# Attention loop: the middle query tiles taken in pairs, with PSUM bank pairs rotating between logits and transposes

## The chip, the core and the metric

One Trainium2 chip, one NeuronCore of it. The engines named here are TensorE (PE in the rows, its weight loads PEld), VectorE (DVE), ScalarE (ACT), GpSimd (POOL) and SyncE (SP, which issues DMAs). The metric is the device time of one execution in microseconds (us), as the median of several runs.

## What is computed

A transformer block: attention with a residual, then a mixture of experts with a residual. Only the attention is touched:

```python
x = x + _layernorm(_L0_attn_ref(_layernorm(x, axis=-1), L0_attn_w_qkv, L0_attn_w_proj, L0_attn_b_proj), axis=-1)
x = x + _layernorm(_L0_ffn_ref(_layernorm(x, axis=-1), ...), axis=-1)
# attention, x is (8, 1024, 256)
qkv = jnp.einsum('bse,he->bsh', x, w_qkv)
q, k, v = jnp.split(qkv, 3, axis=-1)
scores = jnp.einsum('bqh,bkh->bqk', q, k) * scale
probs = jax.nn.softmax(scores, axis=-1)
out = jnp.einsum('bqk,bkh->bqh', probs, v)
out = jnp.swapaxes(out, 1, 2).reshape(Bn, Sn, H)
out = jnp.einsum('bsh,eh->bse', out, w_proj) + b_proj
```

## The kernel before

The program first runs eight attention rounds, one for each batch entry of 1024 tokens (`r` = 0 to 7; rounds 3 to 6 are a hardware loop over one body, the others are written out), and then the mixture of experts. The rounds take the span from about 18 to 564 us. All order is written by hand: each engine runs its own `body(R)` in program order and the engines meet at counting semaphores (`wait(engine, semaphore, value)`).

A round begins on TensorE with 24 matmuls for `tT` (the queries times the folded weights), from round 1 on 48 matmuls of the last round's output projection, and 48 matmuls for V. Then come the eight query tiles of 128 rows. For one query tile `i` the work is a chain over three engines. All products are made of three matmuls (`mm3`: high times high, high times low, low times high), so each result in PSUM is split by ScalarE (high part) and VectorE (low part).

- **logits(i)**: 12 matmuls of 128x512 on TensorE (L60 to L62) into a pair of PSUM banks. Called S below.
- **largest(i)**: VectorE, negated row maximum of the 1024 logits (L710).
- **exp(i)**: ScalarE, exponent with row sum (L555, and a short row that reads the accumulator), into `Pr`.
- **turn(i)**: 8 transposes of 128x128 on TensorE (L442) into a pair of banks. Called P below.
- **hi(i), lo(i)**: ScalarE copies the high part in two halves (L548), VectorE makes the low part in two halves (L723).
- **value product(i)**: 8 matmuls of 128x512 (L453, needs hi(i)) and 8 of 128x256 (L458, needs lo(i)), into `psO` or `psL`. Called H and L below.
- **o_sum(i)** on VectorE (L705), **o_hi(i)** on ScalarE (L543), **o_lo(i)** on VectorE (L716): the output tile, in this order, each waiting for the one before.

Before, logits used `psS` (bank pairs 1 and 0 in turn) and the transposes always used `psPT` (bank pair 2). The steps run one tile at a time, so TensorE's row of work in a round is S0 S1 P0 S2 P1 H0L0 S3 P2 H1L1 S4 P3 H2L2 S5 P4 H3L3 S6 P5 H4L4 S7 P6 H5L5 P7 H6L6 H7L7.

Between the steps each engine does side work of the round:

- ScalarE, rounds 2 to 7: `join` (L487) in steps 2 and 3. Rounds 1 to 7: `norm_y` (L471) in steps 3 and 4.
- VectorE: `ln_y` (statistics of the projected output, rounds 1 to 7) in steps 0 to 2, `gate_scores` (rounds 2 to 7) in step 1, `ln_next` (statistics of the next batch entry, rounds 0 to 6) in steps 2 and 3, `ln_x1` (statistics of x after the attention, rounds 1 to 7) in steps 5 and 6.
- GpSimd: in this order, a chain of small operations after `ln_y` (which lets `norm_y` start), one after `ln_next` (L765 to L775), and then `add_x` (L747), two additions of 1024 columns, of which the first waits for the first `norm_y` and the second for the second. `ln_x1` part 0 waits for the first addition (semaphore `s_x1`), part 1 for the second.
- Round 0 has none of `ln_y`, `norm_y`, `join`, `gate_scores`, `ln_x1`, but splits three shared weights (`shared_hi` on ScalarE, L219, then `shared_lo` on VectorE, L224, which waits for it) in steps 1, 2 and 6, and centres one in step 5.

Of the kernel before, what the change touches and what calls it, by code (L numbers as in the profile page):

```python
# [227 lines left out]
def attention(nc, io, c):  # L228
    with ExitStack() as ctx:
# [75 lines left out]
        def logit_bank(i):  # L305
            return 2 - 2 * (i % 2)
# [60 lines left out]
        def _(pe):  # L367
# [13 lines left out]
            def body(R):  # L381
# [42 lines left out]
                for step in range(NT + 2):  # L424
                    i0, i1, i2 = step, step - 1, step - 2
                    if i0 < NT:
                        b = logit_bank(i0)
                        if i0 < 2:
                            wait(pe, s_vl, 4 * r + 2 * i0 + 2)
                        else:  # L430
                            wait(pe, s_exp, 8 * r + i0 - 1)
                        for n in range(2):
                            for kk in range(KD):
                                w = [tT[z][:, kk, i0 * P:(i0 + 1) * P] for z in (0, 1)]
                                x = [xnT[z][:, kk, n * 512:(n + 1) * 512] for z in (0, 1)]
                                i = mm3(pe, psS[:, b + n, :], w[0], w[1], x[0], x[1], kk == 0, kk == KD - 1)
                        i.then_inc(s_s, 1)
                    def turn_p():
                        wait(pe, s_exp, 8 * r + i1 + 1)
                        wait(pe, s_ptl, 2 * (8 * r + i1))  # L440
                        for t in range(NT):
                            i = pe.transpose(psPT[:, t * P:(t + 1) * P], Pr[:, i1 % 2, t * P:(t + 1) * P], c.ident[:, :])  # L442
                            if t % 4 == 3:
                                i.then_inc(s_t, 1)

                    def output(ts):
                        if ts[0] == 0:
                            wait(pe, s_pth, 2 * (8 * r + i2 + 1))
                            wait(pe, s_os, 8 * r + i2 - 1)
                            if i2 == 0:  # L450
                                wait(pe, s_vl, 4 * (r + 1))
                        for t in ts:
                            pe.matmul(output_bank(i2)[:, :], PT[0][:, i2 % 2, t, :], V_both[:, t, :, :].rearrange("p z d -> p (z d)"),  # L453
                                      start=(t == 0), stop=False)
                        for t in ts:
                            if t == 0:
                                wait(pe, s_ptl, 2 * (8 * r + i2 + 1))
                            i = pe.matmul(output_bank(i2)[:, 0:D], PT[1][:, i2 % 2, t, :], V[0][:, t, :], start=False, stop=(t == NT - 1))  # L458
                        i.then_inc(s_pv, 1)

                    if 0 <= i1 < NT:
                        turn_p()
                    if i2 >= 0:
                        output(range(NT))
# [3 lines left out]
        def _(a):  # L468
# [45 lines left out]
            def body(R):  # L514
# [21 lines left out]
                for step in range(NT + 3):  # L536
                    i0, i1, i3 = step, step - 1, step - 3
                    if i3 >= 0:
                        if i3 == 0:
                            wait(a, s_y, 4 * r)  # L540
                        wait(a, s_ri, 8 * r + i3 + 1)
                        wait(a, s_os, 8 * r + i3 + 1)
                        a.activation(O[0][:, i3, :], Osum[:, i3 % 2, :], ACT.Copy, scale=rinv[:, i3:i3 + 1]).then_inc(s_oh, 1)  # L543
                    if 0 <= i1 < NT:
                        wait(a, s_pv, 8 * r + i1 - 1)
                        for h in range(2):
                            wait(a, s_t, 2 * (8 * r + i1) + h + 1)
                            a.activation(PT[0][:, i1 % 2, 4 * h:4 * h + 4, :],  # L548
                                         psPT[:, h * 512:(h + 1) * 512].rearrange("p (t c) -> p t c", t=4),
                                         ACT.Copy).then_inc(s_pth, 1)  # L550
                    if i0 < NT:
                        wait(a, s_max, 8 * r + i0 + 1)
                        wait(a, s_t, 2 * (8 * r + i0 - 1))
                        b = logit_bank(i0)
                        a.activation(Pr[:, i0 % 2, :], psS[:, b:b + 2, :].rearrange("p a c -> p (a c)"), ACT.Exp,  # L555
                                     bias=negmax[:, i0:i0 + 1], accum_out=rowsum[:, i0:i0 + 1]).then_inc(s_exp, 1)
# [8 lines left out]
                    if R.post and step in (3, 4):  # L565
                        norm_y(r, step - 3)
                    if isinstance(r, int) and r == 0 and step in (1, 2, 6):
                        setup.shared_hi(a, (1, 2, 6).index(step))
            rounds(a, body)

        def aggregate(v, n):
            v.drain()
# [16 lines left out]
        def _(v):  # L589
# [30 lines left out]
            def body(R):  # L620
# [75 lines left out]
                def task(step, side):  # L696
                    if (step, side) in tasks:
                        f, part = tasks[step, side]
                        f(part)
# [1742 lines left out]
```

## Time and profile before

| | us |
|---|---|
| median of 3 runs (1948.04 to 1949.56) | 1948.2 |
| the profiled execution | 1948.25 |
| its span, first to last instruction | 1946.2 |
| PE busy in the span | 1919.5 |
| DVE busy | 1368.9 |
| ACT busy | 1036.9 |
| POOL busy | 521.9 |

Busy times are sums over the whole span. Matmuls overlap in the rows, because the time of one runs from its start to its modelled end, so what tells how fast TensorE goes is the distance from start to start. A round's times are given on the clock of this profile. Round 5, used as the example, has its first logits at 374.84 us and hands over to round 6 at 426.41 us.

### The profile page before, as it was taken

Reading aid. Unit: us, or ns where it says so; the run is one execution under the profiler, and the core shown is the slowest. Engines: PE = TensorE matmul, PEld = TensorE weight load, DVE = VectorE, ACT = ScalarE, POOL = GpSimd, SP = SyncE. Lnnn points to the kernel's source line nnn. Section 1 sums busy time; section 2 is a strip of 40 time slices with the busy share of each in tenths; the row PEclk is TensorE's granted clock in tenths of the full one; section 3 lists DMA queues with packets and bytes.
Section 4 is the critical chain, followed back from the end, with each engine's and each line's share of the span. In section 5 each row is a group of like instructions: output and inputs, shape, how many; then the busy total and the mean of one; then the engine's idle time right before and its main releaser. Section 6 shows DMA issues by size and latency. Waiting matters only on the chain.

```text
span 1946.2 us, 29069 instructions
## 1 busy us (share of the span) xinstructions
PE 1919.5 (99%) x10608; PEld 1647.2 (85%) x10608; DVE 1368.9 (70%) x2619; ACT 1036.9 (53%) x1929; POOL 521.9 (27%) x611
## 2 busy tenths in 40 slices
PE   8999999999999999999999999999999999999996
PEld 6888888888888888888888888888888888888886
DVE  6777787777776888767677777656565756565647
ACT  5457576675655445445454544545454545455455
POOL 0031132033030000322432333243234323432146
PEclk9999999999999999999999999999999999999998
DMA  3113323324244111444434443444434443434566
GB/s 131 55 33 101 86 100 109 97 78 139 52 157 155 66 61 43 136 82 104 92 89 106 94 99 81 107 87 110 87 97 99 91 105 92 105 85 107 152 216 173
DMA packets 153338, 197.37 MB, mean 101 GB/s; under 512 B 104449, under 2 KB 121089, under 8 KB 145153
## 3 DMA queue, kind: packets, MB, share of 16 engines
q1 hardware_dynamic: 127824, 158.00, 26.1%
q0 software_dynamic: 25392, 37.77, 12.2%
q8 instruction: 74, 1.21, 0.2%
q14 instruction: 48, 0.39, 0.1%
HBM read 114.38 MB, written 59.34 MB: 89 GB/s over the span
## 4 chain that ended last, share of the span: by engine, by line
PE 66%; POOL 2%; DVE 1%; DMA 1%; issue 0%; ACT 0%; DVEq 0%; POOLq 0%
PE mo_psD L1637 12%; PE mo_psG L60 7%; PE mo_psU L60 7%; PE mo_psG L61 7%; PE mo_psG L62 7%; PE mo_psU L62 7%; PE mo_psU L61 7%; PE mo_psD L1642 6%; PE mo_psD L60 1%; PE mo_psD L61 1%; PE mo_psD L62 1%; DMA out_dram<-mo_F 1%; POOL mo_H_lo L2296 1%; PE mo_psX L1359 1%; POOL mo_rs L2306 0%
## 5 line engine op out<-in xcount | busy, mean ns | idle before, releaser
L1774 ACT ACTIVATE mo_HF<-mo_psG 128x512 f32<-128x512 f32 x320 | 191.8, 599 | 375.9 <-PE mo_psU L62 344.2
L2278 POOL DMA_INDIRECT ACC<-OUT,IDX x128 | 201.7, 1576 | 623.8 <-DVE OUT L2069 612.3
L1986 DVE TENSOR_TENSOR mo_HF<-mo_psU,mo_HF 128x512 f32<-128x512 f32 x320 | 220.4, 689 | 187.1 <-ACT mo_HF L1774 180.4
L1637 PE MATMUL mo_psD<-wd,mo_H_hi 128*128 128x512 f32 x1024 | 256.3, 392 | 0.3 <-DVE OUT L2069 0.3
L60 PE MATMUL mo_psG<-mo_XT_hi,wg_hi 128*128 128x512 f32 x640 | 253.7, 396 | 0.6 <-DVE mo_HF L1986 0.5
L60 PE MATMUL mo_psU<-mo_XT_hi,wu_hi 128*128 128x512 f32 x640 | 249.9, 390 | 0.0
L61 PE MATMUL mo_psG<-mo_XT_lo,wg_hi 128*128 128x512 f32 x640 | 249.8, 390 | 0.0
L62 PE MATMUL mo_psG<-mo_XT_hi,wg_lo 128*128 128x512 f32 x640 | 249.3, 390 | 0.0
L62 PE MATMUL mo_psU<-mo_XT_hi,wu_lo 128*128 128x512 f32 x640 | 249.0, 389 | 0.0
L61 PE MATMUL mo_psU<-mo_XT_lo,wu_hi 128*128 128x512 f32 x640 | 249.0, 389 | 0.0
L1637 PEld LDWEIGHTS mo_psD<-wd,mo_H_hi 128*128 128x128 f32 x1024 | 185.7, 188 | 35.2 <-DVE OUT L2069 0.5
L1896 DVE TENSOR_TENSOR mo_H_lo<-mo_HF,mo_H_hi 128x512 fp32r<-128x512 f32 x304 | 207.8, 683 | 0.0
L1733 ACT ACTIVATE mo_H_hi<-mo_HF 128x512 fp32r<-128x512 f32 x318 | 198.0, 623 | 8.5 <-DVE mo_HF L1986 8.5
L2069 DVE SCALAR_TENSOR_TENSOR OUT<-mo_psD,mo_TW,OUT 128x256 f32<-128x256 f32 x128 | 61.9, 484 | 185.9 <-ACT OUT L1832 185.9
L1832 ACT ACTIVATE OUT<-mo_psD,mo_TW 128x256 f32<-128x256 f32 x128 | 60.8, 475 | 239.7 <-PE mo_psD L1642 239.7
L1642 PEld LDWEIGHTS mo_psD<-wd,mo_H_lo 128*128 128x128 f32 x1024 | 141.1, 189 | 10.6
L1642 PE MATMUL mo_psD<-wd,mo_H_lo 128*128 128x256 f32 x1024 | 144.1, 284 | 0.0
L60 PEld LDWEIGHTS mo_psG<-mo_XT_hi,wg_hi 128*128 128x128 f32 x640 | 120.2, 188 | 27.8 <-DVE mo_HF L1986 4.3
L62 PEld LDWEIGHTS mo_psG<-mo_XT_hi,wg_lo 128*128 128x128 f32 x640 | 120.1, 188 | 25.7
L60 PEld LDWEIGHTS mo_psU<-mo_XT_hi,wu_hi 128*128 128x128 f32 x640 | 120.1, 188 | 25.3
L62 PEld LDWEIGHTS mo_psU<-mo_XT_hi,wu_lo 128*128 128x128 f32 x640 | 120.1, 188 | 25.1
L61 PEld LDWEIGHTS mo_psU<-mo_XT_lo,wu_hi 128*128 128x128 f32 x640 | 120.2, 188 | 24.8
(356 smaller groups left out, 3981.6 us busy)
## 6 DMA issues: line engine op xcount, KB each, us to landing
X1a<-wg_in SPq DMA_DIRECT2D x16, 1024.0 KB, 4.8
X1a<-wu_in SPq DMA_DIRECT2D x16, 1024.0 KB, 4.9
X1a<-wd_in SPq DMA_DIRECT2D x16, 1024.0 KB, 4.8
XN<-XG SPq DMA_DIRECT2D x8, 1088.0 KB, 4.1
X<-x_in SPq DMA_DIRECT2D x8, 1024.0 KB, 5.4
out_dram<-X SPq DMA_DIRECT2D x8, 1024.0 KB, 6.3
XN2T<-xn2T SPq DMA_DIRECT2D x8, 1024.0 KB, 5.1
X1a<-xt_in SPq DMA_DIRECT2D x7, 1024.0 KB
```

The lines of the kernel that those rows point to most:

```text
L60: pe.matmul(out, w_hi, x_hi, start=first, stop=False)
L61: pe.matmul(out, w_hi, x_lo, start=False, stop=False)
L62: return pe.matmul(out, w_lo, x_hi, start=False, stop=last)
L1637: pe.matmul(psD[:, t % 2, :], hidden(b, it)[0][:, t * P:(t + 1) * P], wd_both[:, it, :, :].rearrange("p z d -> p (z d)"), start=(it == 0), ...
L1642: i = pe.matmul(psD[:, t % 2, 0:D], hidden(b, it)[1][:, t * P:(t + 1) * P], wd[0][:, it, :], start=False, stop=(it == n - 1))
L1733: a.activation(hidden(b, it)[0], HF[:, it % 2, :], ACT.Copy).then_inc(s_hhi, 1)
L1774: a.activation(HF[:, it % 2, :], psG[:, it % 2, :], ACT.Gelu).then_inc(s_gelu, 1)
L1832: i = a.activation(OUT[:, t, :], psD[:, t % 2, 0:D], ACT.Copy, scale=scale)
L1896: v.tensor_tensor(lo, HF[:, it % 2, :], hi.bitcast(F32), ALU.subtract).then_inc(s_hlo, 1)
L1986: v.tensor_tensor(HF[:, it % 2, :], psU[:, it % 2, :], HF[:, it % 2, :], ALU.mult).then_inc(s_mul, 1)
L2069: v.scalar_tensor_tensor(OUT[:, t, :], psD[:, t % 2, D:2 * D], TW[n % 2][:, 4 * tb + t:4 * tb + t + 1], OUT[:, t, :], ALU.mult, ALU.add).t ...
L2278: g.indirect_dma_start(out=io["ACC"], out_offset=bass.IndirectOffsetOnAxis(ap=c.IDX[:, n, 4 * tb + t:4 * tb + t + 1], axis=0), in_=OUT[:, ...
```

## The change

The order inside a round is written out anew on TensorE, ScalarE and VectorE; the bank pair of each logits and each transpose comes from a table. Nothing is computed differently and no operation is added or removed. The middle query tiles go in pairs. TensorE's row of work is now S0 S1 P0 S2 H0L0 P1 P2, then S3 S4 H1L1 H2L2 P3 P4, then S5 S6 H3L3 H4L4 P5 P6, then S7 H5L5 P7 H6L6 H7L7. Logits use bank pairs 1 0 1 1 2 2 0 0, transposes 2 2 0 0 1 1 2 2. With it the waits change: S4 and S6 now wait for lo(1) and lo(3) (`s_ptl`), because they write the banks that these read; of the transposes only the odd ones wait for the lo of the tile before.

The side work keeps its step numbers as arguments of `tasks` (ScalarE) and `task` (VectorE), with one change of place: `ln_x1` part 0 stands alone in step 5, parts 1 and 2 in step 6.

```diff
-        def logit_bank(i):
-            return 2 - 2 * (i % 2)
+        LOGIT_BANKS = [bank_pairs[i] for i in (1, 0, 1, 1, 2, 2, 0, 0)]
+        TURN_BANKS = [bank_pairs[i] for i in (2, 2, 0, 0, 1, 1, 2, 2)]
...
+                def logits(i):
+                    if i < 2:
+                        wait(pe, s_vl, 4 * r + 2 * i + 2)
+                    elif i in (4, 6):
+                        wait(pe, s_ptl, 2 * (8 * r + i - 2))
+                    else:
+                        wait(pe, s_exp, 8 * r + (1 if i == 2 else i))
...
+                def turn_p(i):
+                    wait(pe, s_exp, 8 * r + i + 1)
+                    if i in (1, 3, 5, 7):
+                        wait(pe, s_ptl, 2 * (8 * r + i))
...
+                logits(0)
+                logits(1)
+                turn_p(0)
+                logits(2)
+                output(0)
+                turn_p(1)
+                turn_p(2)
+                for i in (3, 5):
+                    logits(i)
+                    logits(i + 1)
+                    output(i - 2)
+                    output(i - 1)
+                    turn_p(i)
+                    turn_p(i + 1)
+                logits(7)
+                output(5)
+                turn_p(7)
+                output(6)
+                output(7)
             rounds(pe, body)
...
+                exp(0)
+                turned_p(0)
+                exp(1)
+                tasks(1)
+                exp(2)
+                tasks(2)
+                o_hi(0)
+                turned_p(1)
+                turned_p(2)
+                tasks(3)
+                for i in (3, 5):
+                    exp(i)
+                    tasks(4 if i == 3 else 6)
+                    exp(i + 1)
+                    o_hi(i - 2)
+                    o_hi(i - 1)
+                    turned_p(i)
+                    turned_p(i + 1)
+                exp(7)
+                tasks(7)
+                o_hi(5)
+                turned_p(7)
+                tasks(8)
...
             rounds(a, body)
...
-                              (5, 0): (ln_x1, 0), (5, 1): (ln_x1, 1), (6, 0): (ln_x1, 2)}
+                              (5, 0): (ln_x1, 0), (6, 0): (ln_x1, 1), (6, 1): (ln_x1, 2)}
...
+                largest(0)
+                task(0)
+                largest(1)
+                turned_p(0)
+                task(1)
+                if R.gate:
+                    gate_scores()
+                largest(2)
+                task(2)
+                o_sum(0)
+                o_lo(0)
+                turned_p(1)
+                turned_p(2)
+                task(3)
+                for i in (3, 5):
+                    largest(i)
+                    if i == 5:
+                        task(6)
+                    largest(i + 1)
+                    if i == 3:
+                        task(5)
+                    o_sum(i - 2)
+                    o_lo(i - 2)
+                    o_sum(i - 1)
+                    o_lo(i - 1)
+                    turned_p(i)
+                    turned_p(i + 1)
+                largest(7)
+                task(7)
+                o_sum(5)
+                o_lo(5)
+                turned_p(7)
...
             rounds(v, body)
```

The first place is TensorE in round 2, after the transposes of tile 0 and the logits of tile 2. Before:

```order
L442 MATMUL psPT<-ident,Pr 128x128 [waits s_ptl,s_exp]
L442 MATMUL psPT<-ident,Pr 128x128 x7
L453 MATMUL psO<-V,PT_hi 128x512 [waits s_vl,s_os,s_pth]
L453 MATMUL psO<-V,PT_hi 128x512 x7
L458 MATMUL psO<-V,PT_lo 128x256 [waits s_ptl]
L458 MATMUL psO<-V,PT_lo 128x256 x7
```

After, on the same engine at the same place:

```order
L453 MATMUL psO<-V,PT_hi 128x512 [waits s_vl,s_os,s_pth]
L453 MATMUL psO<-V,PT_hi 128x512 x7
L457 MATMUL psO<-V,PT_lo 128x256 [waits s_ptl]
L457 MATMUL psO<-V,PT_lo 128x256 x7
L443 MATMUL psPT<-ident,Pr 128x128 [waits s_ptl,s_exp]
L443 MATMUL psPT<-ident,Pr 128x128 x7
L443 MATMUL psS<-ident,Pr 128x128 [waits s_exp]
L443 MATMUL psS<-ident,Pr 128x128 x7
```

The value product of tile 0 moved ahead of the transposes of tile 1, and the transposes of tile 2 follow at once, ahead of the logits of tile 3.

The second place is VectorE in round 2, from largest(2) (the first row) to the low part of tile 2 (the last row). Before:

```order
L710 TENSOR_REDUCE negmax<-psS 128x1 [waits s_s]
L720 RECIPROCAL rinv<-rowsum 128x1 [waits s_exp]
L723 TENSOR_TENSOR PT_lo<-psPT,PT_hi 128x512 [waits s_pth] x2
L574 BN_AGGR mv<-st 128x2 x8
L581 BN_STATS st<-X 128x6 [waits s_x]
L581 BN_STATS st<-X 128x6 x3
L705 TENSOR_REDUCE Osum<-psO 128x256 [waits s_pv]
L710 TENSOR_REDUCE negmax<-psS 128x1 [waits s_s]
L716 SCALAR_TENSOR_TENSOR O_lo<-Osum,rinv,O_hi 128x256 [waits s_oh]
L720 RECIPROCAL rinv<-rowsum 128x1 [waits s_exp]
L723 TENSOR_TENSOR PT_lo<-psPT,PT_hi 128x512 [waits s_pth] x2
```

After:

```order
L759 TENSOR_REDUCE negmax<-psS 128x1 [waits s_s]
L615 BN_AGGR mv<-st 128x2 x8
L622 BN_STATS st<-X 128x6 [waits s_x]
L622 BN_STATS st<-X 128x6 x3
L749 TENSOR_REDUCE Osum<-psO 128x256 [waits s_pv]
L754 SCALAR_TENSOR_TENSOR O_lo<-Osum,rinv,O_hi 128x256 [waits s_oh]
L764 RECIPROCAL rinv<-rowsum 128x1 [waits s_exp]
L767 TENSOR_TENSOR PT_lo<-psPT,PT_hi 128x512 [waits s_pth] x2
L764 RECIPROCAL rinv<-rowsum 128x1 [waits s_exp]
L767 TENSOR_TENSOR PT_lo<-psS,PT_hi 128x512 [waits s_pth] x2
```

The low part of tile 1 moved behind o_sum(0) and o_lo(0), and stands together with that of tile 2.

The third place is VectorE later in round 2, around the wait for GpSimd's addition (`s_x1`). Before, the rows end with the second part of `ln_x1`:

```order
L705 TENSOR_REDUCE Osum<-psO 128x256 [waits s_pv]
L710 TENSOR_REDUCE negmax<-psS 128x1 [waits s_s]
L716 SCALAR_TENSOR_TENSOR O_lo<-Osum,rinv,O_hi 128x256 [waits s_oh]
L720 RECIPROCAL rinv<-rowsum 128x1 [waits s_exp]
L723 TENSOR_TENSOR PT_lo<-psPT,PT_hi 128x512 [waits s_pth] x2
L581 BN_STATS st<-X 128x6 [waits s_x1]
L581 BN_STATS st<-X 128x6 x3
L581 BN_STATS st<-X 128x6 [waits s_x1]
L581 BN_STATS st<-X 128x6 x3
```

After, from largest(3) on:

```order
L759 TENSOR_REDUCE negmax<-psS 128x1 [waits s_s]
L759 TENSOR_REDUCE negmax<-psPT 128x1 [waits s_s]
L622 BN_STATS st<-X 128x6 [waits s_x1]
L622 BN_STATS st<-X 128x6 x3
L749 TENSOR_REDUCE Osum<-psL 128x256 [waits s_pv]
L754 SCALAR_TENSOR_TENSOR O_lo<-Osum,rinv,O_hi 128x256 [waits s_oh]
L749 TENSOR_REDUCE Osum<-psO 128x256 [waits s_pv]
L754 SCALAR_TENSOR_TENSOR O_lo<-Osum,rinv,O_hi 128x256 [waits s_oh]
L764 RECIPROCAL rinv<-rowsum 128x1 [waits s_exp]
L767 TENSOR_TENSOR PT_lo<-psS,PT_hi 128x512 [waits s_pth] x2
```

The wait for `s_x1` stood behind the low part of tile 4 and now stands behind largest(4), ahead of o_sum(1) and of everything for tiles 1 to 4 that follows on VectorE.

## Rows read from the trace of the kernel before

**Rows 1.** The page: busy time of the engines, and the chain that ended last.

```profile
PE 1919.5 (99%) x10608; PEld 1647.2 (85%) x10608; DVE 1368.9 (70%) x2619; ACT 1036.9 (53%) x1929; POOL 521.9 (27%) x611
...
PE 66%; POOL 2%; DVE 1%; DMA 1%; issue 0%; ACT 0%; DVEq 0%; POOLq 0%
```

**Rows 2.** Timeline, TensorE, round 5: start us, us, then the operation.

```profile
380.46 1.09 PE L442 MATMUL psPT<-ident,Pr 128*128 128x128 f32 x8
381.31 0.48 PE L60 MATMUL psS<-xnT_hi,tT_hi 128*128 128x512 f32 x1
...
384.14 1.03 PE L442 MATMUL psPT<-ident,Pr 128*128 128x128 f32 x8
384.93 2.08 PE L453 MATMUL psO<-V,PT_hi 128*128 128x512 f32 x8
386.85 1.13 PE L458 MATMUL psO<-V,PT_lo 128*128 128x256 f32 x8
387.81 0.39 PE L60 MATMUL psS<-xnT_hi,tT_hi 128*128 128x512 f32 x1
...
390.56 1.03 PE L442 MATMUL psPT<-ident,Pr 128*128 128x128 f32 x8
391.35 2.08 PE L453 MATMUL psL<-V,PT_hi 128*128 128x512 f32 x8
...
423.60 2.01 PE L453 MATMUL psL<-V,PT_hi 128*128 128x512 f32 x8
425.44 1.13 PE L458 MATMUL psL<-V,PT_lo 128*128 128x256 f32 x8
```

**Rows 3.** Timeline, ScalarE, round 5: exp(0), exp(2), first `join`, o_hi(0).

```profile
379.12 1.12 ACT L555 ACTIVATE Pr<-psS,negmax 128x1024 f32<-128x1024 f32 x1 [3.20 <-DVE negmax L710]
...
386.82 1.12 ACT L555 ACTIVATE Pr<-psS,negmax 128x1024 f32<-128x1024 f32 x1 [0.95 <-DVE negmax L710]
...
387.92 2.58 ACT L487 ACTIVATE xn2T<-xn_turned 128x1024 uint16<-128x1024 uint16 x2
390.77 0.51 ACT L543 ACTIVATE O_hi<-Osum,rinv 128x256 fp32r<-128x256 f32 x1 [0.27 <-DVE Osum L705]
```

**Rows 4.** Timeline, VectorE, round 5: lo(1), `ln_next`, largest(4), `ln_x1`, o_sum(5), o_lo(5).

```profile
386.77 1.27 DVE L723 TENSOR_TENSOR PT_lo<-psPT,PT_hi 128x512 fp32r<-128x512 f32 x2
...
395.03 0.64 DVE L574 BATCH_NORM_AGGREGATE mv<-st 128x2 f32<-128x6 f32 x8
...
397.18 1.23 DVE L710 TENSOR_REDUCE negmax<-psS 128x1 f32<-128x1024 f32 x1 [0.94 <-PE psS L62]
...
406.58 2.70 DVE L581 BATCH_NORM_STATS2 st<-X 128x6 f32 x8
...
420.46 0.68 DVE L705 TENSOR_REDUCE Osum<-psL 128x256 f32<-128x512 f32 x1
421.78 0.49 DVE L716 SCALAR_TENSOR_TENSOR O_lo<-Osum,rinv,O_hi 128x256 fp32r<-128x256 f32 x1 [0.64 <-ACT O_hi L543]
```

**Rows 5.** Timeline, GpSimd, round 5: first row of the `ln_next` chain, both additions.

```profile
395.76 0.20 POOL L765 TENSOR_TENSOR ve<-mv,eps 128x8 f32<-128x8 f32 x1 [2.58 <-DVE mv L574]
...
399.60 2.41 POOL L747 TENSOR_TENSOR X<-X,X1a 128x1024 f32 x1 [0.39 <-issue]
402.38 2.38 POOL L747 TENSOR_TENSOR X<-X,X1a 128x1024 f32 x1 [0.37 <-ACT X1a L471]
```

**Rows 6.** Timeline, ScalarE and VectorE, round 0: the second shared weight's split.

```profile
43.07 1.05 ACT L219 ACTIVATE wu_hi<-XG 128x1024 fp32r<-128x1024 f32 x1
...
44.15 1.23 DVE L224 TENSOR_TENSOR wu_lo<-XG,wu_hi 128x1024 fp32r<-128x1024 f32 x1 [0.97 <-ACT wu_hi L219]
```

**Rows 7.** Stretches: length, busy us of PE, PEld, DVE, ACT, POOL, then PEclk, DMA, GB/s.

```profile
564.28:566.63 2.35, 0.17 (x2) 0.03 (x1) 1.19 (x3) 0.51 (x1) 0.04 (x1) 1.00 0.00 0
567.50:571.00 3.50, 3.50 (x19) 3.50 (x18) 0.46 (x1) 3.25 (x7) 0.09 (x2) 0.52 0.92 286
615.50:619.00 3.50, 3.50 (x19) 3.50 (x19) 0.38 (x2) 1.76 (x3) 0.00 (x0) 0.53 0.02 5
```

More of the change, by code:

```diff
@@ L423, in body @@
                     i.then_inc(s_v, 1)
[L424 to L464, printed above, removed]
@@ L535, in body @@
                     a.activation(SM[:, :, :], SM[:, :, :], ACT.Exp).then_inc(s_sme, 1)
[L536 to L556, printed above, removed]
@@ L557, in body, with o_hi, tasks @@
+                def o_hi(i):
+                    if i == 0:
+                        wait(a, s_y, 4 * r)
+                    wait(a, s_ri, 8 * r + i + 1)
+                    wait(a, s_os, 8 * r + i + 1)
+                    a.activation(O[0][:, i, :], Osum[:, i % 2, :], ACT.Copy, scale=rinv[:, i:i + 1]).then_inc(s_oh, 1)
+                def tasks(step):
                     if R.gate and step in (2, 3):
@@ L729, in body, with task @@
+                def task(step):
                     if isinstance(r, int) and r == 0 and step in (1, 2, 6):
@@ L732, in body, with o_sum @@
                         setup.center(v)
-                    task(step, 0)
-                    task(step, 1)
-                    if step == 1 and R.gate:
-                        gate_scores()
+                    for side in range(2):
+                        if (step, side) in tasks:
+                            f, part = tasks[step, side]
+                            f(part)
+                def o_sum(i):
+                    wait(v, s_pv, 8 * r + i + 1)
+                    v.tensor_reduce(Osum[:, i % 2, :], output_bank(i)[:, :].rearrange("p (z d) -> p d z", z=2), AX.X,
+                                    ALU.add).then_inc(s_os, 1)
@@ new lines, in turned_p @@
+                def turned_p(i):
+                    wait(v, s_exp, 8 * r + i + 1)
+                    v.reciprocal(rinv[:, i:i + 1], rowsum[:, i:i + 1]).then_inc(s_ri, 1)
+                    for h in range(2):
+                        wait(v, s_pth, 2 * (8 * r + i) + h + 1)
+                        v.tensor_tensor(PT[1][:, i % 2, 4 * h:4 * h + 4, :], TURN_BANKS[i][:, h, :].rearrange("p (t c) -> p t c", t=4),
+                                        PT[0][:, i % 2, 4 * h:4 * h + 4, :].bitcast(F32), ALU.subtract).then_inc(s_ptl, 1)
@@ L737, in _ @@
+                largest(7)
[3 more added lines that the diff above has]
+                turned_p(7)
+                if R.ln_next:
+                    scale_next(1)
+                    scaled_lo(r + 1, (0, 1))
+                o_sum(6)
+                if R.ln_next:
+                    scaled_lo(r + 1, (2, 3))
+                o_lo(6)
+                o_sum(7)
+                o_lo(7)
             rounds(v, body)
```

76 lines of the change are left out of this document (44 added, 32 removed).

## The prediction

> **What bounds the kernel now.** I read the page first. TensorE is busy for 1919.5 of 1946.2 us, and the chain that ended last is TensorE's for 66%, with no other engine above 2% [rows 1]. That share alone doesn't say that TensorE never waits, because matmuls overlap in the rows. So I read next the timeline of TensorE in round 5, for the distance from start to start. One step there is 12 logit matmuls in 2.75 us (387.81 to 390.56), 8 transposes in 0.79 (to 391.35), and a value product of about 1.92 and 0.96 us [rows 2], 6.42 us in all, and the steps from tile 3 to tile 7 repeat with it. Logits that follow logits take 2.73. So TensorE runs back to back, and only the first transposes of a round wait: S0 starts at 374.84 and two logits take 5.46, to 380.30, while P0 starts at 380.46 [rows 2]. The other engines have room: ScalarE waited 0.95 us before exp(2) and VectorE 0.94 us before largest(4) [rows 3, 4]. Anything that makes TensorE wait is therefore paid in full, and anything that lets the others run faster gives nothing.
>
> **What the pairs can give.** The matmuls are the same. Only the changes from one kind to another differ. A first half of a value product behind transposes takes 1.92 (384.93 to 386.85), behind a value product 1.84 (423.60 to 425.44) [rows 2]: 0.08 each, seven times a round before and once now, 0.45 saved. Logits behind a value product cost 0.02 more than 2.73, five times before and never now, 0.10 saved. Logits behind transposes cost 0.10 more (381.31 to 384.14 is 2.83) [rows 2], taken as 0.11 with the other rounds, once before and four times now, 0.33 lost. Net 0.22 us a round, 1.8 us in eight. Two new neighbours are not in the trace. A value product behind logits lies between 1.84 and 1.92; I take 1.84, since both are the same kind of matmul. Transposes behind transposes I take at the 0.79 of transposes behind logits. With the other ends, the gain is gone and 0.6 us is lost.
>
> **What the new order delays.** VectorE, ScalarE and GpSimd work strictly in their written order, so I laid the new order out by hand from the distances in the rows, for a middle round on the clock of round 5. First the distances: exp is ready for TensorE 1.34 us after its start (379.12 to 380.46) and lets ScalarE go on after 1.10 (386.82 to 387.92) [rows 2, 3]. largest takes 1.23, and the next VectorE row can start 1.14 after it; a pair of low parts takes 1.2; o_lo starts 1.32 after o_sum (420.46 to 421.78), because o_hi on ScalarE lies between them, and lets go after 0.4 [rows 4]. The same distances applied to the old order give a round without any wait but the one before P0, as the trace has it.
>
> *P2 waits for exp(2): 0.44 us.* Up to exp(2) nothing changes, as the work ahead of largest(2) on VectorE is the same. exp(2) starts at 386.8 and is ready at 388.1. Before, TensorE had P1, a value product and S3 ahead of P2, and was there at 390.56. Now it has one value product and P1: S2 ends at 384.1, H0L0 2.80, P1 0.79, so it arrives at 387.7.
>
> *S4 waits for lo(1): 0.96 us.* Lo(1) stood at 386.77, directly behind largest(2) [rows 4]. Now o_sum(0) and o_lo(0) come first, and o_lo(0) needs o_hi(0), which stands behind `join` on ScalarE: 387.92 and two of about 1.2 us, so o_hi(0) starts at 390.3, o_lo(0) at 390.85, lo(1) at 391.35 and its second half is ready at 392.7. S3 starts at 388.9 and ends at 391.7.
>
> *S6 waits for lo(3): 3.12 us.* This is the large one. On GpSimd, the chain after `ln_next` begins when VectorE's aggregate is done (395.03, 0.64 long, then 395.76) and leads to the first addition at 399.60, 3.84 us later, which lasts 2.41 [rows 4, 5]. In the new order the aggregate starts 0.3 us later, so the first addition runs from 399.9 to 402.3. Before, VectorE asked for it at 406.58 [rows 4], 4.6 us after it was there (399.60 + 2.41). Now it asks right behind largest(4): largest(3) at 395.9, largest(4) at 397.0, done with at 398.1. VectorE stands for 4.2 us, and queued behind the wait are o_sum(1), o_lo(1), o_sum(2), o_lo(2), lo(3) and lo(4). From 402.3: `ln_x1` part 0 is half of 2.70 (1.33), to 403.7; o_sum(1), o_lo(1), 1.72, to 405.4; o_sum(2), o_lo(2), to 407.1; the small reciprocal; lo(3) halves at 407.2 and 407.8, ready at 408.57. TensorE is done with H1L1 H2L2 P3 P4 S5 at 405.45 and waits for the bank pair that lo(3) reads. Behind S6 the round has slack again. P7 comes only 2.8 us after S7, and largest(7) and exp(7) take 0.2, 1.25 and 1.34, which is the same 2.8: no stall, but nothing to spare.
>
> **The sum.** Rounds 2 to 6 have all three: 4.52 each, less 0.22, is 4.30, or 21.5 for five. Round 1 has no `join` and no `gate_scores`, so all comes earlier by more than the first two waits and only S6's is left, 2.47: net 2.2. Round 7 has no `ln_next`, so GpSimd goes straight to the addition, which then waits for the first `norm_y` (behind both `join`s): P2 0.44, S4 0.96, S6 0.44: net 1.6. Round 0 has the shared weights instead. A split of 1024 columns takes ScalarE 1.05 us and VectorE 1.23, and VectorE's waits for ScalarE's [rows 6]. In task(2) it now stands between largest(2) and o_sum(0), so VectorE waits 2.3 us there for exp(2) and the ScalarE copy behind it: P2 0.33, S4 2.88, P7 0.34: net 3.4. Together 21.5 + 2.2 + 1.6 + 3.4 = 28.7 us. The mixture of experts starts behind the last round's value product as before, so nothing absorbs this.
>
> *The clock.* From 564.28 to 566.63 TensorE stood nearly idle, 2.35 us, with transposes behind, and in the stretch 567.5 to 571 the granted clock is 0.52, which is the lower level of 1.2 GHz for almost all of 3.5 us [rows 7]. That costs up to 3.5 times 0.48, 1.7 us. Seven of the new stalls are at least as long (S4 of round 0, S6 of rounds 1 to 6). The bounds are 0 and 7 x 1.7 = 11.9 us. That one stall had transposes behind it, and mine have logits at once, so not each will be followed by a drop; I take two or three, 4.2 us.
>
> Forecast: 28.7 + 4.2 = 32.9 on 1948.25 of the profiled execution, which is the median of 1948.2 within 0.05: **1981 us**.
>
> **Rivals.**
> *The rotation works as drawn.* If S4 and S6 find their banks free and P2 its exponents, only the 1.8 us of neighbours are left: 1946.4, no measurable change. For it speaks that TensorE had no wait before and the others had room; against it, the 4.6 us by which VectorE's request for the addition was late before, and is early now. The Trainium skill (Perfetto Trace Analysis, section Optimizing Tensor Performance, Matmuls) says that independent groups of matmuls should rotate through different PSUM banks, so that emptying one overlaps the next group. By that rule this rival would hold. The trace of before does not contradict it, but it shows that the emptying engine has other waits in its queue, of which the rule says nothing.
> *The stalls, and no drop of the clock:* 1977. *The stalls, and a drop at each of the seven:* 1989. In the second a slow S6 also makes largest(6) late by a few tenths.
> *The other side.* The trace has a second stretch at the lower clock soon after the first, 615.5 to 619, about as long [rows 7]. If the new timing moves both starts so that neither drops, 2 x 1.7 and the 1.8 make 5.2 us: 1943. This needs the waits to be absent as well; the point from which it decides is that P2, S4 and S6 wait for less than 3.4 us in all eight rounds together.
>
> **How the numbers follow.** Forecast with two to four drops (1979 to 1985) 0.5; none or one 0.22; five or more 0.14; rotation as drawn 0.06; smaller stalls than worked out, for 1952 to 1972, 0.05; the other side 0.03. About 0.2%, or 4 us, is what a measurement of this kernel can tell from no change. So faster 0.03, same 0.06, slower 0.91. The range goes from 1972, five below the case without drops for errors in the distances, to 1991, two above the case with all.
>
> **What would show it.** In the new trace TensorE's starts in rounds 2 to 6 should show P2 late by 0.4 us, S4 by 1.0 and S6 by 3.1; VectorE should be idle some 4.2 us before `ln_x1` part 0, released by GpSimd's addition (L821); each round should last about 4.3 us longer than 69.0 (374.84 to 443.83, from first logits to first logits), round 1 2.2, round 0 3.4. Right behind S6 the granted clock tells about the drops. I am wrong if VectorE doesn't wait for the addition, or if S6 starts right behind S5.

## The result

| | before | changed |
|---|---|---|
| median | 1948.21 us (1948.04 to 1949.56) | 1986.96 us (1984.21 to 1988.04) |
| the profiled execution, its span | 1948.25, 1946.2 | 1987.87, 1985.8 |
| PE busy in the span | 1919.5 | 1934.0 |
| mean granted clock of TensorE | 0.996 | 0.991 |

The ratio is 1.0196, 95% interval 1.0184 to 1.0208. The changed kernel is 38.75 us slower, the forecast was 32.9 (1981, range 1972 to 1991). The traces used below are each of one execution, which need not be the one with the median time.

### The profile after

The page, parts 1 and 4, as in [rows 1]: TensorE's work is the same in count, and the chain that ended last is still TensorE's for 66%.

```profile
PE 1934.0 (97%) x10608; PEld 1655.1 (83%) x10608; DVE 1371.7 (69%) x2619; ACT 1035.1 (52%) x1929; POOL 522.4 (26%) x611
...
PE 66%; DVE 2%; ACT 0%; DVEq 0%; issue 0%; POOL 0%; ACTq 0%; POOLq 0%
```

That part looks almost as before and says nothing of the cause. The list of waits does. TensorE's in the attention (18 to 606 us; engine, line waited for: us in total, times, longest):

```profile
PE psS L60 <- DVE PT_lo L767: 16.7, 7, 3.1
```

A second row of the same kind, for logits into `psPT`, has 7.3 us, seven times, 2.7 at most. TensorE's timeline of round 5 shows where these lie, and is read by starts against [rows 2]. P1 and P2, S3, S4, H1, P3 and P4, S5, S6, H3:

```profile
411.66 1.03 PE L443 MATMUL psPT<-ident,Pr 128*128 128x128 f32 x8
412.89 1.09 PE L443 MATMUL psS<-ident,Pr 128*128 128x128 f32 x8 [0.19 <-ACT Pr L553]
413.74 0.48 PE L60 MATMUL psS<-xnT_hi,tT_hi 128*128 128x512 f32 x1
...
417.50 0.50 PE L60 MATMUL psPT<-xnT_hi,tT_hi 128*128 128x512 f32 x1 [0.78 <-DVE PT_lo L767]
...
420.36 1.98 PE L453 MATMUL psL<-V,PT_hi 128*128 128x512 f32 x8
...
425.95 1.91 PE L443 MATMUL psS<-ident,Pr 128*128 128x128 f32 x16
427.62 0.48 PE L60 MATMUL psPT<-xnT_hi,tT_hi 128*128 128x512 f32 x1
...
433.66 0.53 PE L60 MATMUL psS<-xnT_hi,tT_hi 128*128 128x512 f32 x1 [3.05 <-DVE PT_lo L767]
434.00 0.61 PE L61 MATMUL psS<-xnT_lo,tT_hi 128*128 128x512 f32 x1
434.41 0.63 PE L62 MATMUL psS<-xnT_hi,tT_lo 128*128 128x512 f32 x1
...
438.12 1.98 PE L453 MATMUL psL<-V,PT_hi 128*128 128x512 f32 x8
```

- P1 and P2 take 2.08 us from start to start (411.66 to 413.74). A pair that waits for nothing takes 1.67 (P3 and P4, 425.95 to 427.62). So P2 is 0.41 late.
- S3 to S4 is 3.76 where 12 logit matmuls behind transposes take 2.83 (381.31 to 384.14 in [rows 2]): S4 is 0.93 late.
- S5 to S6 is 6.04, and S5 too stands behind transposes: S6 is 3.21 late, and it waited for lo(3).
- S4 itself takes 2.86 (417.50 to 420.36), where logits behind logits without a wait take 2.72 or 2.73. So logits that start after a wait cost 0.13 more.
- S6 itself takes 4.46 (433.66 to 438.12), with most of its matmuls 0.41 to 0.43 apart instead of 0.23: 1.73 more than 2.73. Of that 0.13 is the start after a wait, as in S4, and 1.6 is the price of the lower clock.

Why lo(3) is late stands in VectorE's and GpSimd's timelines of round 5: largest(4), `ln_x1` part 0, o_sum(1), o_lo(1), lo(3), and the two additions.

```profile
421.76 1.22 DVE L759 TENSOR_REDUCE negmax<-psPT 128x1 f32<-128x1024 f32 x1
427.21 1.41 DVE L622 BATCH_NORM_STATS2 st<-X 128x6 f32 x4 [4.23 <-POOL X L821]
428.53 0.68 DVE L749 TENSOR_REDUCE Osum<-psL 128x256 f32<-128x512 f32 x1
429.84 0.76 DVE L754 SCALAR_TENSOR_TENSOR O_lo<-Osum,rinv,O_hi 128x256 fp32r<-128x256 f32 x1 [0.64 <-ACT O_hi L568]
...
432.32 1.29 DVE L767 TENSOR_TENSOR PT_lo<-psS,PT_hi 128x512 fp32r<-128x512 f32 x2
```
```profile
420.82 0.20 POOL L839 TENSOR_TENSOR ve<-mv,eps 128x8 f32<-128x8 f32 x1 [4.20 <-DVE mv L615]
...
424.62 4.72 POOL L821 TENSOR_TENSOR X<-X,X1a 128x1024 f32 x2 [0.39 <-issue]
```

VectorE stands for 4.23 us behind largest(4) for the first addition, which began 3.80 us after the chain's first row (424.62 - 420.82) as in [rows 5], and all that TensorE needs next is queued behind that wait.

The granted clock, in stretches (length, busy us of PE, PEld, DVE, ACT, POOL, then PEclk, DMA share, GB/s): in S4 of round 0, in S6 of round 1, in S6 of round 5, and in the mixture of experts.

```profile
49.60:53.10 3.50, 3.50 (x15) 2.89 (x16) 3.43 (x16) 0.09 (x1) 0.19 (x1) 1.00 0.02 5
133.90:137.40 3.50, 3.50 (x10) 2.69 (x10) 3.43 (x12) 1.21 (x2) 0.00 (x0) 0.55 0.23 44
...
434.00:437.40 3.40, 3.40 (x9) 2.62 (x8) 3.33 (x8) 1.21 (x2) 0.00 (x0) 0.50 0.34 77
652.50:659.30 6.80, 6.80 (x34) 6.80 (x34) 2.40 (x7) 2.36 (x4) 0.00 (x0) 0.50 0.01 4
```

There is such a stretch of 3.4 us at the 1.2 GHz level in S6 of each of rounds 1 to 6, beginning 0.1 to 1.1 us after its first matmul, and none in rounds 0 and 7. In the experts before had two of 3.4 us [rows 7], and the changed kernel has one of 6.8, which costs the same. This is the profiled execution. The four on record lie between 1984.21 and 1988.04 us at mean granted clocks of 0.993 to 0.990, so the number of such stretches need not be six in each.

Round by round, from first logits to the next round's first matmul, the changed kernel takes longer by 3.16, 3.59, 5.53, 6.37, 6.30, 6.33 and 6.34 us, and by 1.75 in round 7. That is 39.4, and the end of the attention is indeed 39.2 later (605.85 against 566.63). Behind it the two traces differ by 0.4 us.

### The profile page after: what moved, and what is told of

Read it like the earlier page. It is cut to its first block, busy times and chain, and to the rows that moved or that the text cites. A ratio compares the mean times of both kernels' runs of the same rounds, so it can differ in the third digit from the quotient of the medians.

```text
span 1985.8 us, 29062 instructions
## 1 busy us (share of the span) xinstructions
PE 1934.0 (97%) x10608; PEld 1655.1 (83%) x10608; DVE 1371.7 (69%) x2619; ACT 1035.1 (52%) x1929; POOL 522.4 (26%) x611
## 4 chain that ended last, share of the span: by engine, by line
PE 66%; DVE 2%; ACT 0%; DVEq 0%; issue 0%; POOL 0%; ACTq 0%; POOLq 0%
PE mo_psD L1711 12%; PE mo_psG L60 7%; PE mo_psU L60 7%; PE mo_psG L61 7%; PE mo_psG L62 7%; PE mo_psU L61 7%; PE mo_psU L62 7%; PE mo_psD L1716 6%; PE mo_psD L60 1%; PE mo_psD L61 1%; PE mo_psD L62 1%; PE mo_psX L1433 1%; DVE mo_F L2033 0%; DVE mo_junk_v L2015 0%; DVE mo_HF L2060 0%
```

## Experiments

The theory: the pair puts VectorE's request for GpSimd's first addition in front of lo(3), S6 waits for lo(3), and the stall of S6 brings the lower clock with it. P2 and S4 have small waits from ScalarE's and VectorE's side work in steps 1 and 2, and round 0 has one from the shared weights. The rivals: pairs and rotated banks cost something of their own, or VectorE is simply too full. Where nothing else is said, an edit is on the changed kernel. The kernel before ran beside them at 1947.2 to 1948.1 us.

### x1_late: the statistics of x behind lo(3) and lo(4)

```
-                               (5, 0): (ln_x1, 0), (6, 0): (ln_x1, 1), (6, 1): (ln_x1, 2)}
+                               (6, 0): (ln_x1, 1), (6, 1): (ln_x1, 2)}
...
                     turned_p(i)
                     turned_p(i + 1)
+                    if R.post and i == 3:
+                        ln_x1(0)
```

> The kernel after with one edit: ln_x1 part 0 (which waits for GpSimd's first addition) stands behind lo(4) on VectorE and no longer behind largest(4). Theory (the early wait for the addition is what holds S6): S6 starts right behind S5 in rounds 1 to 7, VectorE has no wait for the addition, no stall of 2.4 us or more is left but S4 of round 0, so none of the six stretches at the lower clock. Left are P2, S4 of rounds 2 to 7, round 0 and a small wait of P7 of 0.2 us: 11.5 us over the kernel before, 1959.7. Rival (the two output tiles that now stand ahead of lo(3) on VectorE are enough to make S6 late; the addition only adds its own 1.3 us of VectorE work): S6 still waits some 1.8 us in each of rounds 1 to 6, about 1970.

1964.75 us (1962.31 to 1968.38), ratio 1.0094 (1.0078 to 1.0111). Moving one task of 1.4 us took back 22.2 of the 38.75 us. The attention of the trace has no stretch at the lower clock left. The time is 5 above the expectation. The traced execution took 1962.31 us, 2.6 above it; the one of 1968.38 had a mean granted clock of 0.993 against 0.996, and where its clock was lower is not known. TensorE's waits say where part of the 2.6 is:

```profile
PE psPT L60 <- DVE PT_lo L767: 7.3, 7, 2.7
PE psS L60 <- DVE PT_lo L767: 2.7, 6, 0.6
```

The first row is S4, as in the changed kernel. The second should have gone: S6 still waits 0.5 to 0.6 us in rounds 3 to 6. VectorE's timeline in round 5, o_lo(1), o_sum(2), o_lo(2), and GpSimd's additions beside it:

```profile
410.91 0.71 DVE L754 SCALAR_TENSOR_TENSOR O_lo<-Osum,rinv,O_hi 128x256 fp32r<-128x256 f32 x1 [2.54 <-ACT O_hi L568]
411.55 0.68 DVE L749 TENSOR_REDUCE Osum<-psO 128x256 f32<-128x512 f32 x1
412.86 1.29 DVE L754 SCALAR_TENSOR_TENSOR O_lo<-Osum,rinv,O_hi 128x256 fp32r<-128x256 f32 x1 [0.64 <-ACT O_hi L568]
```
```profile
408.94 4.93 POOL L823 TENSOR_TENSOR X<-X,X1a 128x1024 f32 x2 [0.39 <-issue]
```

o_lo takes 0.49 us before [rows 4]. Here o_lo(2) takes 1.29 and ends at 414.15, 0.28 us after the additions (408.94 + 4.93 = 413.87). I had not thought of that; two runs below test it.

### x1_mid: the same task between o_lo(1) and o_sum(2)

```
                     o_sum(i - 2)
                     o_lo(i - 2)
+                    if R.post and i == 3:
+                        ln_x1(0)
                     o_sum(i - 1)
```

> The kernel after with ln_x1 part 0 moved by two operations only, behind o_lo(1) and ahead of o_sum(2). It grades the stall: S6 should wait 1.4 us in rounds 2 to 6, 0.7 in round 1 and 1.25 in round 7, in place of 3.1, 2.5 and 0.4. Theory on the clock (only a stall of some 2.4 us or more brings the lower level): no stretch at the lower clock in the attention, 19.1 us over the kernel before, 1967.3. Rival (every repeated stall at this place brings it): six stretches, 1.7 us each, 1977.5.

1969.69 us (1968.40 to 1970.19), ratio 1.0111 (1.0094 to 1.0128). VectorE no longer waits for the addition, but the task's own time is in front of lo(3), and S6 waits up to 1.5 us (6.9 in seven waits). None of these is followed by the lower clock. The trace has one stretch of it in the attention, in round 0's S4. The 2.4 us that the text above takes as the least stall is not a bound: in the changed kernel the clock also fell behind round 1's stall of 1.79 us.

### pool_first: the first addition ahead of GpSimd's chain

```
+                if R.post:
+                    add_x(r, 0)
                 if R.ln_next:
                     chain(0, r + 1, s_r1)
                 if R.post:
-                    add_x(r)
+                    add_x(r, 1)
```

> The kernel after, VectorE untouched; on GpSimd the first addition stands ahead of the chain for the next batch entry, so it starts when the first norm_y is done. Theory (the addition's time decides): it is there 2.6 us earlier, at about 399.7 on the old clock of round 5, S6 waits 0.44 us in rounds 2 to 6 and not at all in round 1: 12.8 us over the kernel before, 1961, without the drops of the clock. Rival (VectorE's queue of output tiles decides, not the addition): as the kernel after, 1987.

1969.25 us (1968.27 to 1973.33), ratio 1.0110 (1.0093 to 1.0126). VectorE's order is that of the changed kernel; its wait for the addition falls from 4.23 to 1.84 us and 17.7 us come back. So it is this wait and not the amount of VectorE's work. (`add_x` is called here for one half at a time.) But the time is 8 above the expectation: S6 waits 1.7 us where I expected about 0.4. VectorE and GpSimd in round 5, `ln_x1` part 0 and o_lo(2), and the second addition:

```profile
414.82 1.41 DVE L622 BATCH_NORM_STATS2 st<-X 128x6 f32 x4 [1.84 <-POOL X L821]
...
419.18 1.82 DVE L754 SCALAR_TENSOR_TENSOR O_lo<-Osum,rinv,O_hi 128x256 fp32r<-128x256 f32 x1 [0.64 <-ACT O_hi L568]
```
```profile
418.33 2.40 POOL L821 TENSOR_TENSOR X<-X,X1a 128x1024 f32 x1 [0.33 <-issue]
```

o_lo(2) takes 1.82 us and ends at 421.00, 0.27 after the addition's end (420.73). The 1.33 us beyond its normal 0.49 are the missing part of S6's wait, 6.6 us over rounds 2 to 6. The traced execution took 1973.33 us.

### single_x1_early: the old order, with only the early request

On the kernel before, `ln_x1` part 0 directly behind largest(4), one tile at a time:

```
-                            (5, 0): (ln_x1, 0), (5, 1): (ln_x1, 1), (6, 0): (ln_x1, 2)}
+                            (5, 1): (ln_x1, 1), (6, 0): (ln_x1, 2)}
...
+                    if R.post and step == 4:
+                        ln_x1(0)
```

> The kernel before, tiles one by one, with only ln_x1 part 0 asked for early: behind lo(3) is too late for this, so it stands behind largest(4) and ahead of o_lo(1), as in the kernel after. Theory (the place of the wait costs time in either order): VectorE waits for the addition, lo(3) comes late and P4, which writes the same banks, waits 1.8 us in rounds 1 to 6: 11.1 us over the kernel before, 1959.3, no lower clock. Rival (only the pairs make the wait expensive): 1948.2.

1974.44 us (1972.01 to 1974.81), ratio 1.0139 (1.0122 to 1.0155): without a pair and without rotated banks, 26 us of loss. So the early request alone does it. TensorE, P4 in round 5, and VectorE and GpSimd beside it:

```profile
421.04 1.97 PE L442 MATMUL psPT<-ident,Pr 128*128 128x128 f32 x8 [2.77 <-DVE PT_lo L725]
```
```profile
416.85 1.41 DVE L581 BATCH_NORM_STATS2 st<-X 128x6 f32 x4 [3.75 <-POOL X L749]
418.18 1.55 DVE L718 SCALAR_TENSOR_TENSOR O_lo<-Osum,rinv,O_hi 128x256 fp32r<-128x256 f32 x1
```
```profile
417.07 2.36 POOL L749 TENSOR_TENSOR X<-X,X1a 128x1024 f32 x1 [0.43 <-ACT X1a L471]
```

It lost 15 us more than expected, for two reasons: again o_lo ends 0.30 after an addition (419.73 against 419.43), which makes the stall 2.8 us instead of 1.84, and four of the six stalls are followed by the lower clock. Of the rounds with stalls of 2.8 us, those with it (4 to 6) take 73.3 to 73.6 us, those without (2 and 3) 71.9 and 72.0, so a stretch costs 1.3 to 1.6. The traced execution took 1972.01 us; the other three took 1974.3 to 1974.8 at a mean granted clock of 0.991 against 0.992.

### x1_late_pieces: GpSimd's addition in eight instructions

On x1_late, to test what holds o_lo:

```
-                    x = X[:, (r - 1) % XS, 4 * h:4 * h + 4, :]
-                    g.tensor_tensor(x, x, Y[:, 4 * h:4 * h + 4, :], ALU.add).then_inc(s_x1, 1)
+                    for t in range(4 * h, 4 * h + 4):
+                        x = X[:, (r - 1) % XS, t, :]
+                        last = g.tensor_tensor(x, x, Y[:, t, :], ALU.add)
+                    last.then_inc(s_x1, 1)
```

> As x1_late, and GpSimd adds X1a to X in eight instructions of 128x512 instead of two of 128x2048 elements, with the same two signals. Theory (VectorE's O_lo, which reads two SBUF tiles, is held until the GpSimd addition that is under way ends): in x1_late O_lo of the pair's second tile took 1.29 us instead of 0.48, ending 0.28 us after the addition (408.94 to 413.87), and logits 6 then waited 0.6 us in six rounds. With pieces of about 0.6 us O_lo can be held for one piece at most, 0.3 us in the middle of its place, so it takes 0.5 to 1.1 us, and 0.3 to 0.6 us of each of the six waits goes: 2 to 3.5 us off 1964.75, 1961 to 1963. Rival (O_lo is late for a reason of VectorE's own, such as the reduction before it): O_lo stays at 1.29 us and the time at 1964.75. On the other side: the pieces cost GpSimd 6 more starts and VectorE's statistics of X wait for them, over 1966.

(That text has the sizes wrong: a piece is 128x256 elements, an addition 128x1024.) 1962.99 us (1961.47 to 1964.57), ratio 1.0074 (1.0060 to 1.0087). o_lo(2) in round 5, and the pieces:

```profile
413.27 1.02 DVE L754 SCALAR_TENSOR_TENSOR O_lo<-Osum,rinv,O_hi 128x256 fp32r<-128x256 f32 x1 [0.64 <-ACT O_hi L568]
```
```profile
409.59 5.99 POOL L824 TENSOR_TENSOR X<-X,X1a 128x256 f32 x8 [0.39 <-issue]
```

It gets in while the eight are still under way (they end at 415.58), so it waits for one instruction and not for the sum. S6's wait is gone but for one of 0.5 us, and a middle round takes 70.75 us instead of 71.25. The median moved by 1.8 only, at the lower edge of what was expected, and the two kernels' executions overlap; it is the rounds of the traces that show the gain.

### x1_late_tiny_add: nearly no addition

On x1_late, GpSimd adds 8 columns of one tile for each of its signals, so X1 lacks nearly all of the attention's output:

```
-                    x = X[:, (r - 1) % XS, 4 * h:4 * h + 4, :]
-                    g.tensor_tensor(x, x, Y[:, 4 * h:4 * h + 4, :], ALU.add).then_inc(s_x1, 1)
+                    x = X[:, (r - 1) % XS, 4 * h:4 * h + 1, 0:8]
+                    g.tensor_tensor(x, x, Y[:, 4 * h:4 * h + 1, 0:8], ALU.add).then_inc(s_x1, 1)
```

> As x1_late, but GpSimd adds only 8 columns of one tile for each of its two signals, so the sum X + X1a is left out and the output of the later parts is of other numbers. Theory (O_lo is held by a GpSimd instruction with two SBUF inputs that is under way): every O_lo of rounds 2 to 6 takes 0.48 us, logits 6 wait no more, and a middle round goes from 71.25 to 70.65 us: six times 0.6 off 1964.75, 1961. Rival (it is the place in VectorE's queue): O_lo keeps 1.29 us and the round 71.25.

1961.38 us (1959.29 to 1962.46), ratio 1.0068 (1.0051 to 1.0085). A middle round takes 70.4 to 70.5 us, no wait of S6 is left, and o_lo(2) of round 5 is back at its normal time although its place in VectorE's queue is the same:

```profile
412.09 0.49 DVE L754 SCALAR_TENSOR_TENSOR O_lo<-Osum,rinv,O_hi 128x256 fp32r<-128x256 f32 x1 [0.64 <-ACT O_hi L568]
```

In three of the rounds the first o_lo takes 0.72 or 0.73. GpSimd then runs a multiplication for the gate beside it (0.40 us, two SBUF inputs), which in round 4 ends 0.28 us before it does.

### after_tiny_add: the changed kernel, with the small addition

> The changed kernel, with the same small addition; the sum X + X1a is left out. Its orders on VectorE and TensorE are untouched. Theory (S6 waits because VectorE stands for the first addition): the statistics of X can start when GpSimd's chain of small operations is over, 424.85 instead of 427.1 on the clock of round 5. VectorE then stands 2.0 us instead of 4.2 and S6 waits 0.8 us instead of 3.05 in rounds 2 to 6. No stall of 0.8 us is followed by the lower clock, so its 1.7 us go too in six rounds: 1986.96 - 6 x 2.25 - 6 x 1.7 = 1963. If the lower clock stays though the stall is short: 1973. Rival (S6 is late for the order of VectorE's work, not for the addition): 1985 or more.

1963.43 us (1961.72 to 1964.86), ratio 1.0078 (1.0062 to 1.0095). VectorE's wait ahead of `ln_x1` part 0 and TensorE's ahead of S6, round 5:

```profile
411.07 1.40 DVE L622 BATCH_NORM_STATS2 st<-X 128x6 f32 x4 [2.05 <-POOL X L821]
```
```profile
417.25 0.50 PE L60 MATMUL psS<-xnT_hi,tT_hi 128*128 128x512 f32 x1 [0.59 <-DVE PT_lo L767]
```

23.5 us come back with the orders of TensorE, VectorE and ScalarE untouched. The addition's duration and the clock behind it carry most of the loss, and S6 at 0.6 us brings no lower clock.

### x1_gate_join: the two small waits of a round

On x1_late:

```
                 task(1)
-                if R.gate:
-                    gate_scores()
                 largest(2)
                 task(2)
                 o_sum(0)
+                if R.gate:
+                    gate_scores()
                 o_lo(0)
...
                 tasks(1)
+                if R.gate:
+                    join(r, 0)
                 exp(2)
```

The first `join` is taken out of `tasks(2)`.

> As x1_late, and the sums for the gate stand behind o_sum(0) on VectorE instead of ahead of largest(2), and the first join stands ahead of exp(2) on ScalarE, not behind it. Theory (the two small waits of each middle round come from what stands ahead of turned_p(1) and of exp(2), as in the prediction's steps for P2 and S4): P2's 0.4 us and nearly all of S4's 0.8 us go in rounds 2 to 7 (S4 keeps round 0's 3 us, where shared_lo stands ahead), so 2 + 5 us off 1964.75: 1957.5. The 0.6 us of logits 6 stay. Rival (each wait is replaced by another one of the pair, since both queues are full there): 1963 to 1966. On the other side: the join now holds exp(2) and P2 waits 1.3 us longer, 1971.

1953.82 us (1953.48 to 1956.71), ratio 1.0031 (1.0020 to 1.0042). P2's wait has left the list, S4's is there once (2.7 us, round 0), S6 waits four times for up to 0.4. A middle round is 69.6 us. It came out 3.7 under the expectation: 10.9 us came back for the 7 that I had counted. I had taken S4's wait from the idle column, 0.78. By starts round 5 gives 0.93, and S4 itself takes 2.72 instead of 2.85 when it doesn't start after a wait. S6's wait gets shorter too: S5 to S6 is 3.52 in x1_late (411.95 to 415.47) and 3.37 here. With P2's 0.4 these make 1.6 us a round.

### best, and best_pieces: round 0 as well

On x1_gate_join. In round 0 ScalarE splits the first shared weight ahead of turned_p(0), and VectorE the second behind o_sum(0) and the third behind largest(6); in the others the aggregate of x stands behind largest(6) too. Their old places are taken out, which isn't shown:

```
                 exp(0)
+                tasks(1)
                 turned_p(0)
                 exp(1)
-                tasks(1)
...
                 o_sum(0)
+                if isinstance(r, int) and r == 0:
+                    setup.shared_lo(v, 1)
...
                     largest(i + 1)
+                    if i == 5 and R.post:
+                        ln_x1(2)
+                    if i == 5 and isinstance(r, int) and r == 0:
+                        setup.shared_lo(v, 2)
```

> As x1_gate_join, and in round 0 the first three tasks of the shared weights stand behind the work that the pair waits for (ScalarE's ahead of turned_p(0), VectorE's behind o_sum(0) and behind largest(6)), and so does the aggregate of X. Theory (all waits that the pairs bring are queue orders of ScalarE and VectorE, and what the pairs save at TensorE's block neighbours, 0.22 us a round, stays): round 0's 3.1 us go as well, and only the 0.6 us of logits 6 held by the addition stay in six rounds: 1948 + 3.6 - 1.8 + about 1.5 = 1951. Rival (the pairs save nothing, and the moved tasks stall the next step): 1955 to 1958.

1950.39 us (1948.92 to 1952.11, 11 runs), ratio 1.0010 (1.0001 to 1.0019). A middle round takes 69.6 us, 0.6 more than before, and S6 waits up to 0.4 us in four of them. With the addition in eight instructions on top (best_pieces):

> As best, with the addition in eight instructions. Theory: the last 0.6 us of six rounds go too, and the kernel is 0.1% under the kernel before: 1947 (1946 to 1949). Rival (a pair costs something that isn't a wait): 1951 or more. With the addition in pieces of no use, as best.

1948.29 us (1946.75 to 1949.65, 11 runs), ratio 0.9999 (0.9990 to 1.0008). TensorE's only wait for VectorE or ScalarE left in the attention is

```profile
PE psS L60 <- DVE PT_lo L769: 0.2, 1, 0.2
```

So the pairs and the rotated banks cost nothing that can be measured by themselves: all 39 us come from how the other engines' work stands around them, the last 2 from the length of GpSimd's instructions. The same reordering without pairs was not run; the kernel before has no wait for VectorE or ScalarE in its attention that it could take away but the one ahead of P0. Nor do they bring anything that can be measured; no version beats the kernel before.

## Why the prediction was right, and where it missed

**TensorE's waits, term by term, for round 5.** P2 0.44 forecast and 0.41 measured; S4 0.96 and 0.93; S6 3.12 and 3.21. VectorE's wait for the addition was put at 4.2 and is 4.23. The S6 term was short by 0.1 us. It lacked that o_lo(1) holds VectorE 0.28 us longer than o_lo(2) does (0.76 against 0.48): GpSimd runs an instruction of 0.46 us with two SBUF inputs beside it, which ends at 430.32, and o_lo(1) ends at 430.60. No term stood for the 0.13 us that S4 and S6 each take more when they start after a wait, 0.27 in a middle round.

By rounds, with each stretch at the lower clock taken off at 1.6 us: round 0 was put at 3.4 and is 3.2 (its terms add up to 3.33, and P7's 0.34 didn't come), round 1 at 2.2 and is 2.0, round 2 at 4.3 and is 3.9, rounds 3 to 6 at 4.3 and are 4.7 to 4.8, round 7 at 1.6 and is 1.75. Together 29.8 us, against the forecast's 28.7. That these sums are so near is in part luck, since rounds 0 to 2 came out shorter and the others longer.

**The term that was mis-sized is the clock.** The step "I take two or three, 4.2 us" failed. Six stalls were followed by the lower clock, all S6, and six times 1.6 is 9.6: that is 5.4 us more than forecast. With the 1.1 us of the stalls it makes the 6.5 by which the attention's 39.4 us exceed 32.9 in the traces; by the medians the whole miss is 5.9. Its price was nearly right (1.6 measured on S6 of round 5, 1.7 forecast). The reason given for few of them, that transposes had stood behind the stall of before and logits would stand behind these, fell: all six had logits behind them. One that I had counted among the seven, S4 of round 0 (2.68 us idle), had none. The example from which I took the price, the idle time ahead of the experts' first transposes (2.18 us by the idle column), is in all twelve traces, and the clock fell at its end or within 1.0 us behind it in six of them.

What the traces say of when the clock falls: behind idle times of 0.5 to 1.73 us of TensorE inside the attention, never (S6 in x1_late, x1_mid, pool_first and after_tiny_add, nineteen times). Behind 1.79 us in round 1, 2.38 in round 2 and 3.05 to 3.12 in rounds 3 to 6 of the changed kernel, each time. Behind 2.4 to 2.8 us in single_x1_early, four of six, and of its four stalls of 2.77 to 2.79 us one was not followed by it. At round 0's S4, with the same 2.68 us idle in eight traces, six times, and not in the changed kernel and x1_late. So the length of a stall doesn't settle it alone, and what else does stays open: no run was made that moves one and the same stall in time. For a forecast, most of such stalls of about 2 us and more was the better guess than a third of them.

**The gain.** The neighbours were forecast at -0.22 us a round, and best_pieces has middle rounds of 69.1 us against 69.0 before. In its round 4, from start to start, a first half behind logits takes 1.82 us (forecast 1.84), four times, and the first halves save 0.55 in all. But two groups of transposes in a pair take 1.66 to 1.67 and not 1.58, as their sixteen matmuls start 0.11 apart throughout, while a group that another kind follows gives way after 0.79: the step "Transposes behind transposes I take at the 0.79" failed, and the transposes cost 0.31 more than before in all. Logits and second halves cost 0.1 more, and S6's last small wait, with its start after it, costs 0.2. Without that last wait a saving of 0.14 us is left, 1 us in eight rounds, below what can be told.

**The rivals.** "The rotation works as drawn" stood on the premise that the other engines had room. They have it, but not in the right place of their queues. best_pieces is that rival, built: 1948.3, where it was put at 1946.4. The rule named there, from the Trainium skill (Perfetto Trace Analysis, Optimizing Tensor Performance, Matmuls), speaks of banks; in this trace S6 started when lo(3) had read its bank, and lo(3) was late for another engine's sake. The stalls with a drop at each of the seven, 1989, were nearest to what came, 1986.96; the chance of 0.14 for five or more was too small. The range held the result because it reached to a drop at every stall.

## What to carry to other kernels

When work is taken in pairs, each step that releases the pair inherits the waits of everything that stands ahead of it in its engine's queue: look for requests to a third engine (here VectorE's for GpSimd) that came late enough before to find their answer ready, and ask whether they still do. A side task of 1.4 us that waits 4 us in front of the critical step cost 22 us, the lower clock behind it included, in six rounds, and moving it behind that step cost nothing that shows. Where such a stall of 2 to 3 us repeats in a kernel whose TensorE is busy throughout, price the lower clock behind most of them, not behind a few: here it followed ten of thirteen in the changed kernel and single_x1_early.

## What the runs showed of the hardware

**An operation of VectorE with two SBUF inputs is held while GpSimd runs one.** o_lo reads `Osum` and `O_hi`, both in SBUF, and takes 0.48 us. Started during an addition of GpSimd (2.4 us) it took 1.29, 1.55, 1.82 and 2.01 us, for example. In the twelve traces it took 0.6 us or more 91 times, and each time it ended 0.28 or 0.29 us after a GpSimd operation did (0.27 to 0.30 by the rounded rows above). GpSimd waits as well: an addition that started while an o_lo was under way took 2.56 to 2.59 us, the others 2.36 to 2.41. The second half of x1_late's pair and the tiny addition show both sides in the same place: 1.29 and 0.49. In the same windows the low parts, which read PSUM and SBUF, keep 1.26 to 1.29 for two, and the row maxima, which read PSUM, 1.2. The statistics of x, one SBUF input, keep 1.4. The Trainium skill (SBUF — State Buffer, section SBUF: two separate sides) states that VectorE and GpSimd share a port pair as an exclusive lock for a whole instruction, also for a VectorE operation with two SBUF inputs against a GpSimd operation that reads SBUF. By that rule this had to be, and all traces agree, with 0.28 or 0.29 us after the end of the other. The trace of before holds the row that would have told it, an o_lo of round 7, beside an addition:

```profile
536.20 2.27 DVE L716 SCALAR_TENSOR_TENSOR O_lo<-Osum,rinv,O_hi 128x256 fp32r<-128x256 f32 x1
```
```profile
535.79 2.40 POOL L747 TENSOR_TENSOR X<-X,X1a 128x1024 f32<-128x1024 f32 x1 [4.74 <-ACT X1a L471]
```

It made TensorE wait for nothing there. Durations of one row, taken from a place where the other engine was idle, hide it; the longest row of a group is worth a look as much as its mean.
